# Layer 1's fp32 rows of `up` between the first job's products, layer 2's odd rows in fp32 side by side, and the scales' floor by a reduction

## The reference

```python
approx_up = x @ up_w.T;  delta = x @ gate_w.T - local_point
out = approx_up @ local_approx_output.T
for m in 1..6:                              # terms
    out += (exp(log|delta|*m - c[m]) * sign * approx_up * keep) @ fuse_weight[:, :, m-1].T
out += (silu(x @ ffn_gate_w.T) * (x @ ffn_up_w.T)) @ ffn_down_w.T      # F = 1248
x = layernorm(x + out)
dq = code[searchsorted(bounds, w / absmax)] * absmax     # blocks of 64, for w1, w2, w3
x = layernorm(x + (silu(x @ dq1.T) * (x @ dq2.T)) @ dq3.T)             # F = 1376
```

## Time and profile before

| what | value |
|---|---|
| median of three runs | 410.64 us (410.25 to 410.75) |
| the profiled execution, its own time | 410.27 us |
| its span, first to last instruction | 408.2 us |
| TensorE busy | 399.9 us, 98% |
| VectorE, ScalarE, GpSimd busy | 79%, 65%, 71% |
| granted TensorE clock, mean | 0.997 of full |

### The profile page before, as it was taken

How to read it: one execution, slowest core, us unless ns; L and a number is a source line. 1 busy time by engine, 2 the same in 40 slices (tenths; PEclk the granted TensorE clock), 3 DMA queues, 4 the chain that set the end, 5 groups by cost and what they waited for, 6 DMA issues and landing times.

```text
span 408.2 us, 5342 instructions
## 1 busy us (share of the span) xinstructions
PE 399.9 (98%) x1762; PEld 325.8 (80%) x1762; DVE 324.3 (79%) x385; ACT 267.0 (65%) x372; POOL 289.8 (71%) x228
## 2 busy tenths in 40 slices
PE   8999999999999999999999999999999999999993
PEld 6767888888888888888888888888888877888872
DVE  4539889789889996999969799887789989925035
ACT  5574676686685847466955668887769777732613
POOL 0177998986978499737992465799999998954330
PEclk9999999999999999999999999999999999999998
DMA  8993111000104362003052000000000000000202
GB/s 276 406 408 126 53 22 51 28 26 0 53 20 116 92 213 71 26 0 104 1 167 112 0 2 0 0 2 0 2 2 0 2 0 0 2 1 0 104 0 103
DMA packets 10010, 26.42 MB, mean 65 GB/s; under 512 B 1248, under 2 KB 1632, under 8 KB 9728
## 3 DMA queue, kind: packets, MB, share of 16 engines
q1 hardware_dynamic: 9552, 25.30, 17.9%
q10 hardware_dynamic: 432, 0.79, 0.7%
HBM read 23.99 MB, written 2.10 MB: 64 GB/s over the span
## 4 chain that ended last, share of the span: by engine, by line
PE 95%; DVE 1%; POOL 1%; ACT 1%; issue 0%; POOLq 0%; DVEq 0%; ACTq 0%
PE PS L1292 31%; PE PS L1294 31%; PE PS L1293 31%; PE PS L1426 1%; PE PS L1330 1%; PE PS L1420 1%; POOL level L1217 1%; DVE h L917 0%; POOLq L262 0%; PE PS L1435 0%; DVE PS L885 0%; ACT side L635 0%; ACT side L597 0%; PE PS L1438 0%; PE PS L1441 0%
## 5 line engine op out<-in xcount | busy, mean ns | idle before, releaser
L1217 POOL TENSOR_SCALAR level<-side 128x1024 f32<-128x1024 int8 (+2 forms) x119 | 129.0, 1084 | 27.7 <-ACT side L597 15.4
L885 DVE TENSOR_TENSOR PS<-PS,level 128x1024 f32<-128x1024 f32 (+2 forms) x102 | 120.1, 1178 | 22.6 <-POOL level L1217 18.8
L1292 PE MATMUL PS<-x_hi,w_hi 128*128 128x512 f32 (+1 forms) x340 | 132.7, 390 | 0.3 <-DVE h L917 0.3
L1294 PE MATMUL PS<-x_hi,w_lo 128*128 128x512 f32 (+1 forms) x340 | 132.4, 389 | 0.0
L1293 PE MATMUL PS<-x_lo,w_hi 128*128 128x512 f32 (+1 forms) x340 | 132.3, 389 | 0.0
L597 ACT ACTIVATE side<-Q 128x1024 int8<-128x1024 f32 (+2 forms) x84 | 80.6, 998 | 22.1 <-DVE PS L881 18.0
L1247 POOL TENSOR_TENSOR l_lo<-h,l_hi 128x512 fp32r<-128x512 f32 (+1 forms) x42 | 57.3, 1374 | 26.5 <-ACT l_hi L597 25.8
L1292 PEld LDWEIGHTS PS<-x_hi,w_hi 128*128 128x128 f32 (+1 forms) x340 | 63.4, 186 | 15.1 <-issue 0.8
L1294 PEld LDWEIGHTS PS<-x_hi,w_lo 128*128 128x128 f32 (+1 forms) x340 | 63.4, 186 | 13.8
L1293 PEld LDWEIGHTS PS<-x_lo,w_hi 128*128 128x128 f32 (+1 forms) x340 | 63.4, 186 | 13.6
L1293 PE MATMUL PS<-x_lo,l_hi 128*128 128x512 f32 (+1 forms) x144 | 56.1, 389 | 0.0
(11 more groups left out here) (103 smaller groups left out, 515.2 us busy)
## 6 DMA issues: line engine op xcount, KB each, us to landing
Q<-w SPq DMA_DIRECT2D x10, 512.0 KB, 13.9
raw<-w_in SPq DMA_DIRECT2D x9, 512.0 KB, 9.9
raw<-w_out SPq DMA_DIRECT2D x13, 256.0 KB, 2.7
raw<-w SPq DMA_DIRECT2D x5, 512.0 KB, 3.9
R<-xN SPq DMA_DIRECT2D x2, 1024.0 KB, 6.4
raw<-w_fuse SPq DMA_DIRECT2D x7, 256.0 KB, 2.5
out<-R SPq DMA_DIRECT2D x7, 256.0 KB, 2.0
h<-xT SPq DMA_DIRECT2D x2, 512.0 KB, 7.0
```

Source lines behind the costliest of these rows:

```text
L885: v.tensor_tensor(total, total, level_of(s), ALU.add).then_inc(s_add, 1)
L1217: g.tensor_scalar(level_of(s), side_of(s), LIMITS[k][1], LIMITS[k][0], ALU.min, ALU.max).then_inc(s_level, 1)
L1292: t_.matmul(dst, a_hi, b_hi, start=start, stop=False)
L1294: return t_.matmul(dst, a_lo, b_hi, start=False, stop=stop)
```

## The change

Layer 1: `project_up` now takes one chunk, and is called after each chunk of `pre` (four blocks of two calls, in the place of one block of eight). Its weights come by a DMA of their own (`up_raw`, 128x256), issued ahead of the second half of `w_pre`; the load of job 0 shrinks by as much.

Layer 2: the odd unit becomes unit 4 (`ODD`), so its pairs are number 8 and 9 of 22. Gate's 96 rows and 32 of up share 128-wide weights (`project_odd`, 12 matmuls for each half), and the other 64 up rows are done by `project_up2` in fp32, side by side, after pair 8's products. For that, the tokens are put together again from `x_hi + x_lo` by four GpSimd additions of 128x2x512 (`join_x`), and 128x256 of the weights are kept in fp32 by one more ScalarE copy. The `up` copies of pairs 8 and 9 come in two pieces (32 and 64 rows).

Scales: the maxima lie beside a constant floor in `floored`, and a `tensor_reduce` over the pairs takes the place of the `tensor_scalar`. All three `SHARE` tables are new.

```diff
@@ load order on SP
                 if c == 2:
+                    sp.dma_start(up_raw, w_in[:, DC * P:2 * DC * REST]).then_inc(s_up_raw, 16)
                     sp.dma_start(w_raw(0)[:, 2 * PRE0:1024], w_pre[:, 2 * PRE0:1024]).then_inc(s_raw[0], 16)
@@ ScalarE
+                    if is_odd(layer, i):
+                        for to, up_rows in parted_up(layer, i):
+                            last = copy(up2[to, k % 2, :], up_rows)
+                        last.then_inc(s_up2, 1)
@@ VectorE, scales
-                v.tensor_scalar(inverse, maxima, TINY, None, ALU.max).then_inc(s_floor, 1)
+                v.tensor_reduce(inverse, pairs, AX_X, ALU.max).then_inc(s_floor, 1)
@@ GpSimd, at pairs 0, 1, 3 and 5 of layer 2
+            def join_x(half, k):
+                pool.wait_ge(s_xl, X_PARTS + TILES * (half + 1))
+                x, hi, lo = (t[:, 2 * k:2 * k + 2, half * HALF:(half + 1) * HALF] for t in (x2_raw, x_hi, x_lo))
+                g.tensor_tensor(x, hi.bitcast(F32), lo.bitcast(F32), ALU.add).then_inc(s_x2raw, 1)
@@ TensorE
+            def project_up2():
+                w = up2_raw.rearrange("p s (k m) -> p k s m", k=2)
+                for c in range(DC):
+                    pe.wait_ge(s_x2raw, 3 + c // 2)
+                    for half in range(2):
+                        last = t_.matmul(PS[half * LEFT:(half + 1) * LEFT, UP_BANK[2], :], w[:, c // 2, c % 2, :],
+                                         x2_raw[:, c, half * HALF:(half + 1) * HALF], start=c == 0, stop=c == DC - 1)
+                return last
...
+                if is_odd(layer, i):
+                    last = project_odd(layer, slot, half, bank)
+                    if layer == 2 and half == 0:
+                        pe.wait_ge(*bank_free(i - 1))
+                        last = project_up2()
@@ TensorE, pre
             for c in range(1, DC):
+                if c == 1:
+                    pe.wait_ge(s_up_raw, 16)
+                project_up(c - 1)
...
+            project_up(DC - 1).then_inc(s_up_made, 1)
```

More of the change, by code:

```diff
@@ L44 @@
 REST, LEFT = F1 % P, 64
-assert 2 * REST - P == LEFT
+assert F2 % P == REST and 2 * REST - P == LEFT
+ODD = 4
+CHUNK_OF = [*range(ODD), C2 - 1, *range(ODD, C2 - 1)]
 KEEP_FROM = 5
@@ L304, in turned, with odd_part @@
             return PS[:, XT_BANK:XT_BANK + 2, :].rearrange("p b n -> p (b n)")[:, 0:unit_width(f)]
+        x2_raw = h[:, 6 * TOK:(6 + DC) * TOK].rearrange("p (c t) -> p c t", c=DC)
+        up2_raw = h[:, 5 * TOK:5 * TOK + DC * LEFT].rearrange("p (s n) -> p s n", s=2)
+        def odd_part(w, first, last):
+            return w.rearrange("p (s n) -> p s n", s=2)[:, :, first:last]
         def term_tile(m, a):
@@ L440, in h_half @@
             view = h[0:job_rows(SEQ[n][1]), c * TOK + a * HALF:c * TOK + (a + 1) * HALF]
[L441 removed]
+            return view, (s_h, 2 * c + a + 1) if layer == 1 else product_made(PAIR2[CHUNK_OF.index(c), a])
         def product_made(i):
@@ L914, in gate_times_up @@
                 dve.wait_ge(s_silu, i + 1 + (2 * C1 if layer == 2 else 0))
-                if layer == 1 and i < 2:
-                    for to, up_rows in parted_up(i):
+                if is_odd(layer, i):
+                    for to, up_rows in parted_up(layer, i):
                         last = v.tensor_tensor(dst[to, :], up_rows, dst[to, :], ALU.mult)
@@ L1314, in project, with project_odd @@
                 return last
-            def project_first(half, bank):
-                wh, wl = (in_slot(w, JOB["in", 0], DC * P).rearrange("p (c m) -> p c m", c=DC) for w in (w_hi, w_lo))
+            def project_odd(layer, slot, half, bank):
+                if layer == 1:
+                    parts = (in_slot(w, slot, DC * P) for w in (w_hi, w_lo))
+                    wh, wl = (w.rearrange("p (c m) -> p c m", c=DC) for w in parts)
+                else:
+                    parts = (in_slot(w, slot, unit_width(ODD)) for w in (w_hi, w_lo))
+                    wh, wl = (odd_part(w, 0, 2 * P).rearrange("p s (k m) -> p k s m", k=2) for w in parts)
@@ L1319, in project_first @@
                 for c in range(DC):
+                    w_h, w_l = ((w[:, c, :] if layer == 1 else w[:, c // 2, c % 2, :]) for w in (wh, wl))
                     xs = slice(half * HALF, (half + 1) * HALF)
-                    last = product(PS[:, bank, :], wh[:, c, :], wl[:, c, :], x_hi[:, c, xs], x_lo[:, c, xs], c == 0,
-                                   c == DC - 1)
-                return last
-            def project_up():
-                w = w_raw(JOB["in", 0])[:, DC * P:2 * DC * REST].rearrange("p (c m) -> p c m", c=DC)
+                    last = product(PS[:, bank, :], w_h, w_l, x_hi[:, c, xs], x_lo[:, c, xs], c == 0, c == DC - 1)
@@ L1332, in project_up @@
+            def project_up(c):
+                w = up_raw.rearrange("p (c m) -> p c m", c=DC)
+                for half in range(2):
+                    pe.wait_ge((s_x, s_xb)[half if c < 2 else 0][c], 16)
+                    last = t_.matmul(PS[half * LEFT:(half + 1) * LEFT, UP_BANK[1], :], w[:, c, :],
+                                     xT_raw[:, c, half * HALF:(half + 1) * HALF], start=c == 0, stop=c == DC - 1)
                 return last
@@ L1335, in pair @@
                 f, half, bank = pair_of(layer, i)
-                m = rows1(f) if layer == 1 else rows(f, F2)
+                m = P
                 if layer == 1:
@@ L1357, in pair @@
                     pe.wait_ge(s_xl, X_PARTS + (TILES if half == 0 and i < 2 else TT))
-                if layer == 1 and i < 2:
-                    last = project_first(half, bank)
-                    if half == 0:
-                        last = project_up()
+                if is_odd(layer, i):
+                    last = project_odd(layer, slot, half, bank)
+                    if layer == 2 and half == 0:
+                        pe.wait_ge(*bank_free(i - 1))
+                        last = project_up2()
                     last.then_inc(s_pair, 1)
@@ L1509, in by_squares @@
         parts = []
-        for f in range(C2):
+        for f in CHUNK_OF:
             rows_ = [w[f * P:(f + 1) * P].reshape(-1, SQ, 2, DC, BLOCK) for w in ws]
+            if f == C2 - 1:
+                gate, up = rows_
+                parts += [x.transpose(3, 1, 2, 0, 4).reshape(P, -1)
+                          for x in (np.concatenate([gate, up[LEFT // SQ:]]), up[:LEFT // SQ])]
+                continue
             parts.append(np.stack(rows_).transpose(4, 2, 0, 3, 1, 5).reshape(P, -1))
```

64 lines of the change are left out of this document (42 added, 22 removed), and 24 rows, old and new, of the table SHARE.

## The result

| kernel | median of the runs | ratio to before, 95% interval |
|---|---|---|
| before | 410.61 us (410.25 to 410.75) | |
| after | 413.17 us (412.49 to 413.60) | 1.0058 (1.0044 to 1.0073) |

A forecast was written before the change was run, and what follows sets the result against it. The prediction took TensorE, busy 399.9 of 408.2 us, to bound the kernel. Its terms, -1.84 + 1.14 - 0.57 = -1.27 us, gave 409.4 us, with a range from 408.1 to 410.9 us.

The forecast's parts named there:

- What bounds the kernel: Whole kernel: TensorE is busy 399.9 of 408.2 us, so only its queue or a new wait there counts.
- The odd job: Layer 2: 24 matmuls and one fp32 block replace 48 matmuls with 96-wide weights, -1.84 us.
- Four blocks: Layer 1's project_up: entering and leaving a block costs 0.38 us, paid four times instead of once, +1.14 us.
- the rival of free blocks: Layer 1: short blocks cost nothing extra, so 408.2 us; chance 0.14.
- The wait at pair 3: Layer 1, 31.38 us: TensorE's wait for VectorE's product goes with the new queues, -0.57 us; 0 if it stays.
- Work off the path: Added work on GpSimd, VectorE and ScalarE, checked mainly in layer 2, fits their slack and adds nothing to the time.
- The join: GpSimd: four additions of 128x1024 at 2.05 us, 8.2 us in all, within its idle time.
- The floor: Scales by tensor_reduce: at most 2.3 us difference on VectorE over the kernel, all beside TensorE.
- GpSimd's lag reaches TensorE: Layer 2: late GpSimd products make TensorE wait 2.1 us at pair 10, sum +0.8 us or worse; chance 0.11.

The follow-up runs named there:

- the kernel with one block: After with before's step tables in layer 1's second stage, and project_up as one block of eight instead of four blocks: 409.45 us (0.9974 to before).

## Why the prediction was wrong, by its own steps

- **What bounds the kernel**: right. TensorE is at 97% and each lost microsecond is a wait of it.
- **The odd job, -1.84**: right. 24 x 0.2266 + 3.79 = 9.23 us against 11.08.
- **Four blocks, +1.14**: right as the price of the blocks themselves, 3 x 0.36 = 1.08 us by their rows; the rival of free blocks falls. The 1.11 us between the medians of the two kernels that differ in nothing else agrees by luck in part, since one block with the new load order waits some 0.6 us in `pre`. The Trainium skill, TensorEngine Tiling (Array Packing), Tiling Modes, Key Properties, says that changing the tiling mode drains TensorE; that every block of after pays its 0.36 us agrees with it.
- **The wait at pair 3, -0.57**: right in size, and it is the tables that buy it. But it is not independent of the term above: with before's tables the wait is 0.29 us with one block and 2.40 with four. "What is late next is nothing that I can find" was the failed search: it went only through pair 3's own neighbourhood.
- **Work off the path, 0**: this is the step that failed. It went through GpSimd's queue from 229 us on, took 15.5 idle microseconds there as room, and asked of the new tables only what they do at pair 3 and at the odd job. Those slacks were real: neither `project_up2` nor pair 10 waits. But dealing all steps anew is an edit at every place where a step stands, and in layer 1's second stage, which has no other edit, it cost 2.61 us. The two stalls there, 0.72 and 1.94 us, are waits for GpSimd's l_lo behind clamps that the new table put in; GpSimd's old table takes both away, and all three old tables bring 2.61 us back. A clamp of 1.04 us ahead of an operand that in before is done 0.80 us ahead of its use was a term, and it was put at nothing.
- **The join**, inside that step: 2.40 us each instead of 2.05, and its harm is not its length but what it pushes GpSimd's clamps beside. 0.47 us of x_lo's wait (the 0.70 us distance) go when the joins and the clamps are moved; a side step ahead of the last silu gives 0.5 more (0.75 less 0.23). Together these are most of what parts 410.56 us from the sum of the terms, 409.35.
- **The floor, 0**: right for before's arrangement and, by 0.88 us, wrong in the kernel with one block. What it is worth in after itself was not run.
- **The rivals**: "GpSimd's lag reaches TensorE" had the right engine and sign, and the wrong place (pair 10). Its 0.11 was, as I see it now, too little for a change that deals three tables anew in a kernel with 0.5 us of waits in it.

In one sum: -1.84 + 1.14 - 0.57 + 1.2 (the waits at 235.56 and 344.67 us, 0.64 and 0.6) + 2.6 (second stage) = +2.5, measured +2.56.

## What to carry to other kernels

Where one engine is busy 97% and others feed it in order, a table that deals work between the feeds is not a detail of the change: go through every place where it differs, and ask of each inserted operation what operand is queued behind it and how long before its use that operand was done. Splice old and new tables at points where their counts agree, and move a step on all its engines at once: a clamp drawn later on GpSimd alone held an addition on VectorE, and with it the w_lo behind that addition. And when two kernels that differ in one thing differ by just what was forecast, look into both traces all the same: here 1.11 us in the medians were 0.49 in the profiled executions, with a wait in one of them that no expectation had.

## What the runs showed of the hardware

A small VectorE operation can be held by GpSimd. The floor's old form takes 128x32 elements from 128x32 in SBUF. With GpSimd idle it takes 0.18 us (at 104.47 us of the kernel below). In VectorE's timeline of the kernel that has it beside the odd job and one block:

```profile
202.51 2.86 DVE L892 TENSOR_SCALAR rcp<-floored 128x32 f32<-128x32 f32 x1
```

and GpSimd's in the same time:

```profile
201.54 1.29 POOL L1280 TENSOR_TENSOR w_lo<-raw,w_hi 128x512 fp32r<-128x512 f32 x1
202.80 1.28 POOL L1291 TENSOR_TENSOR l_lo<-h,l_hi 128x512 fp32r<-128x512 f32 x1
204.04 1.29 POOL L1280 TENSOR_TENSOR x_lo<-raw,x_hi 128x512 fp32r<-128x512 f32 x1
205.41 1.04 POOL L1261 TENSOR_SCALAR level<-side 128x1024 f32<-128x1024 int8 x1
```

It ends at 205.37 us, in the 0.08 us between the third and the clamp: it sat out three operations that follow each other without a gap. That is not what always happens. In before, VectorE's floor at 201.55 us:

```profile
201.55 0.64 DVE L851 TENSOR_SCALAR rcp<-amax 128x32 f32<-128x32 f32 x1
```

and GpSimd's operations beside it, also without a gap:

```profile
200.83 1.29 POOL L1236 TENSOR_TENSOR w_lo<-raw,w_hi 128x512 fp32r<-128x512 f32 x1
202.09 1.29 POOL L1247 TENSOR_TENSOR l_lo<-h,l_hi 128x512 fp32r<-128x512 f32 x1
```

It ends at 202.19 us, just behind the first of them. What decides between the two was not found.

The reduction that replaced it (over 128x64, once 128x32) takes 0.19 to 0.22 us in all six places of after. The plainest pair is at one place of before, first with the old form and then with the reduction as the only edit:

```profile
100.20 1.13 DVE L851 TENSOR_SCALAR rcp<-amax 128x32 f32<-128x32 f32 x1
```

```profile
100.25 0.22 DVE L852 TENSOR_REDUCE rcp<-floored 128x32 f32<-128x64 f32 x1
```

In both a w_lo of GpSimd is running, from 98.89 to 101.29 us and from 98.93 to 101.34; the old form ends at 101.33 us. The 128x2 operations on the statistics show the same (0.17 us with GpSimd idle, 0.61 and 1.04 beside its clamps), and VectorE's reciprocal in between, at 219.85 us, does not (0.17 us beside a clamp).

The Trainium skill, SBUF — State Buffer, section "SBUF: two separate sides", says that VectorE and GpSimd share a pair of ports as an exclusive lock, held for a whole instruction, which VectorE needs for two SBUF inputs (against a GpSimd operation that reads SBUF) or in its two-port modes. These rows agree with it for the held 128x2 product, whose two inputs are in SBUF, and in that a held operation ends with GpSimd's; whether the floor and the 128x2 sum ran in a two-port mode they don't show. What the rows add is that a held operation can lose to several of GpSimd's in a row when they are back to back, and not only to the one that was running.
